# Small causal heads: transposed scores without a mask product, exponentials clipped on VectorE

## What is computed

```python
x = x + _L3_attn_a_ref(_layernorm(x), W_q, b_q, W_k, b_k, W_v, b_v, W_o, b_o)
x = x + _L3_ffn_ref(_layernorm(x), ...)
x = x + _L3_attn_b_ref(_layernorm(x), w_qkv, w_out)
x = x + _L3_ffn_ref(_layernorm(x), ...)

# inside _L3_attn_a_ref (b is the same without biases and rotation)
scores = jnp.einsum('bhtd,bhsd->bhts', q, k)
causal = jnp.tril(jnp.ones((t, t), dtype=bool))
mask = jnp.where(causal, 0.0, -jnp.inf)
probs = jax.nn.softmax((scores + mask) / jnp.sqrt(jnp.float32(dh)), axis=-1)
out = jnp.einsum('bhts,bhsd->bhtd', probs, v)
```

## Time and profile before

| | |
|---|---|
| median of 3 runs | 2899.02 us (2896.28 to 2901.09) |
| profiled execution, its own time | 2887.07 us |
| its span | 2885.8 us |
| mean granted TensorE clock | 0.892 |
| PE busy | 2243.0 us, 78% |
| DVE busy | 1824.5 us, 63% |
| ACT busy | 1345.5 us, 47% |

### The profile page before, as it was taken

The page is one execution under the profiler, slowest core; times in us unless marked ns, Lnnn a source line. Parts: engine busy times, 40 slices in busy tenths (PEclk is TensorE's granted clock), DMA queues, the critical chain, the costliest instruction groups (busy, mean ns, idle before and its releaser), DMA issues.

```text
span 2885.8 us, 40933 instructions
## 1 busy us (share of the span) xinstructions
PE 2243.0 (78%) x15598; PEld 1461.0 (51%) x15598; DVE 1824.5 (63%) x3594; ACT 1345.5 (47%) x2535; POOL 653.7 (23%) x610
## 2 busy tenths in 40 slices
PE   4868738665884887887798599676689889689888
PEld 1222328643872554555497278355454554454554
DVE  6989997898336996996847655663742432642331
ACT  4545313231334886886673564353443353344242
POOL 1737681313023221220091055000100100100000
PEclk9999969877886998998898699678799999899899
DMA  4000037502763111111000000002000000000000
GB/s 150 0 0 0 5 101 211 157 11 91 222 184 102 44 42 26 45 42 50 35 1 1 0 1 1 0 2 82 1 1 1 1 1 8 1 2 1 1 1 8
DMA packets 70709, 117.80 MB, mean 41 GB/s; under 512 B 9617, under 2 KB 46225, under 8 KB 70161
## 3 DMA queue, kind: packets, MB, share of 16 engines
q1 hardware_dynamic: 64112, 104.69, 12.1%
q0 software_dynamic: 4096, 8.40, 0.9%
q10 hardware_dynamic: 2304, 2.10, 0.3%
HBM read 84.61 MB, written 16.78 MB: 35 GB/s over the span
## 4 chain that ended last, share of the span: by engine, by line
PE 33%; DVE 11%; issue 4%; ACT 3%; DMA 1%; SPq 1%; POOL 1%; DVEq 0%; POOLq 0%; ACTq 0%
PE ps L148 29%; PE ps L157 4%; DVE wide_q L188 3%; SPq L231 1%; DMA ring<-lags 1%; DVE outT L194 1%; DVE conv L185 1%; DVE x L179 1%; DVE stats L203 1%; DVE stat L188 1%; POOL long L179 1%; DVE centred L179 0%; ACT L166 0%; ACT L165 0%; ACT k L166 0%
## 5 line engine op out<-in xcount | busy, mean ns | idle before, releaser
L185 DVE SCALAR_TENSOR_TENSOR conv<-conv_in,held_l1a,conv 128x512 f32<-128x512 f32 x288 | 238.0, 846 | 21.0 <-ACT conv L166 18.2
L179 POOL TENSOR_TENSOR long<-long,product 128x512 f32<-128x512 f32 x136 | 167.8, 1277 | 280.8 <-ACT product L166 280.3
L209 POOL MEMSET wide_q<- 128x1536 f32 x8 | 11.0, 1378 | 871.3 <-DVE stream_b L182 813.8
L179 POOL TENSOR_TENSOR part<-state,c_rows 128x512 f32<-128x512 f32 x128 | 161.0, 1284 | 72.3 <-issue 53.2
L179 POOL TENSOR_TENSOR qk<-conv,held_const 128x512 f32<-128x512 f32 x64 | 90.2, 1410 | 343.7 <-DVE conv L185 343.7
L148 PE MATMUL ps<-part,held_const 128*128 128x512 f32 x256 | 147.0, 658 | 13.2 <-POOL part L179 8.4
L188 DVE TENSOR_REDUCE wide_q<-ps 128x4 f32<-128x512 f32 (+1 forms) x128 | 113.8, 952 | 54.9 <-PE ps L148 54.9
L191 DVE TENSOR_TENSOR_SCAN state<-decay,ps 128x512 f32<-128x512 f32 x128 | 146.9, 1194 | 0.0
L166 ACT ACTIVATE probs<-ps 128x768 f32<-128x768 f32 x128 | 96.5, 808 | 91.0 <-PE ps L148 90.8
L166 ACT ACTIVATE grown<-ps,held_route 128x512 f32<-128x512 f32 x92 | 63.2, 687 | 122.9 <-PE ps L148 106.2
L179 DVE TENSOR_TENSOR x<-x,ps 128x512 f32<-128x512 f32 x44 | 30.1, 684 | 138.7 <-PE ps L148 131.6
(11 more groups left out here) (503 smaller groups left out, 6012.1 us busy)
## 6 DMA issues: line engine op xcount, KB each, us to landing
ring_a<-in_experts SPq DMA_DIRECT2D x46, 512.0 KB
ring_b<-in_experts SPq DMA_DIRECT2D x46, 512.0 KB
turned<-conv SPq DMA_DIRECT2D x256, 64.0 KB
ring<-lags SPq DMA_DIRECT2D x64, 128.0 KB
held_l3f<-in_l3f SPq DMA_DIRECT2D x1, 2824.0 KB
xg<-rows_x_a SPq DMA_DIRECT2D x10, 256.0 KB
xg<-rows_x_b SPq DMA_DIRECT2D x10, 256.0 KB
rows_y_a<-y SPq DMA_DIRECT2D x10, 256.0 KB, 5.4
```

Source lines behind the costliest of these rows:

```text
L179: return self.vector(self.real.tensor_tensor(out, a, b, op), columns(out), out, a, b)
L185: return self.vector(self.real.scalar_tensor_tensor(out, a, p, b, first, second), columns(out) + 60, out, a, b)
L209: return self.vector(self.real.memset(out, value), columns(out) // 2, out)
```

## The change

- In the transposed loop the four products `ps<-ident,after` of a unit are gone. The second set of score products closes the accumulation and raises `scores_t` for the odd heads.
- The exponentials of the two diagonal blocks of each head are therefore made without a mask. A new DVE operation after each exponential instruction (two per unit, each on two heads, 128x2x2x128 elements, in place in `probs`) takes the minimum with a constant tile that is 0 where the key is later than the query and 3e38 elsewhere. It raises the new semaphore `hidden`, and the mix waits for `hidden` instead of `exps`.
- In DVE's program the two minima of a unit stand ahead of its copy to `outT`.
- The constant tile is 128 columns more in the load of the group `l3a` (512 to 640 columns).
- The score loop keeps its mask products.

```diff
--- before.py
+++ after.py
@@ -2594,7 +2594,7 @@
     UNITS = GROUPS * SEQS
     KEYS = P + T
     L = Layer(m, NORM + "projected kept blank placed rotated v turned_k k_kept turned_q q_kept scores peak top turned_t "
-              "t_kept scores_t exps mixed mixed_kept oturned inverse normed yturned okept out biased")
+              "t_kept scores_t exps hidden mixed mixed_kept oturned inverse normed yturned okept out biased")
     s = L.s
     a = Arena(m, st.first, st.late_size)
     n_ = normalize(m, st, L, a, x, st.tok[:, :, :], st.xT[:, :])
@@ -2607,6 +2607,12 @@
 
     def unit(u):
         return u // SEQS, u % SEQS
+
+    def hide_later(lane, u, k):
+        yield lane.wait_ge(s.exps, 2 * u + k + 1)
+        diagonal = e.probs[:, u % 2, 2 * k:2 * k + 2, :].rearrange("p h (c n) -> p h c n", n=P)[:, :, 0:3:2, :]
+        keep = m.w.c_seen.unsqueeze(1).unsqueeze(1).to_broadcast([P, 2, 2, P])
+        lane.tensor_tensor(diagonal, diagonal, keep, ALU.min).then_inc(s.hidden)
 
     def tensor(pe):
         yield from n_.tensor(pe)
@@ -2666,16 +2672,12 @@
                           tile_position=(W * j, 0), skip_group_check=True)
             for j in range(HG):
                 r = slice(W * j, W * j + W)
-                pe.matmul(st.ps(j)[:, T:KEYS], b.kT[r, g, at + P:at + T], b.qT[r, g, at + P:at + T], start=False,
-                          stop=False, tile_position=(W * j, 0), skip_group_check=True)
-            for j in range(HG):
-                diagonal = st.ps(j)[:, 0:KEYS + P].rearrange("p (a n) -> p a n", n=T)[:, :, 0:P]
-                mm = pe.matmul(diagonal, m.after[:, :], m.ident16[:, :].unsqueeze(1).to_broadcast([P, 2, P]),
-                               start=False, stop=True, skip_group_check=True)
+                mm = pe.matmul(st.ps(j)[:, T:KEYS], b.kT[r, g, at + P:at + T], b.qT[r, g, at + P:at + T], start=False,
+                               stop=True, tile_position=(W * j, 0), skip_group_check=True)
                 if j % 2:
                     mm.then_inc(s.scores_t)
             yield pe.wait_ge(s.v, 1)
-            yield pe.wait_ge(s.exps, 2 * (u + 1))
+            yield pe.wait_ge(s.hidden, 2 * (u + 1))
             pr = e.probs[:, u % 2, :, :]
             for j in range(HG):
                 pe.matmul(st.ps(0)[W * j:W * j + W, 0:T], b.wide_v[:, TPS * q, HG * g + j, :], pr[:, j, 0:T],
@@ -2783,8 +2785,11 @@
             for i, (at, keys) in enumerate(((0, P), (P, T))):
                 ve.tensor_reduce(b.wide_q[:, TPS * q + i, HG * g:HG * g + HG, D], all_of(keys, at), X, ALU.max,
                                  negate=True).then_inc(s.peak)
+        yield ve.wait_ge(*m.loaded["l3a"])
         for u in range(UNITS):
             g, q = unit(u)
+            for k in range(2):
+                yield from hide_later(ve, u, k)
             yield ve.wait_ge(s.mixed, u + 1)
             ve.tensor_copy(e.outT[:, g, q * T:q * T + T], st.ps(0)[:, 0:T]).then_inc(s.mixed_kept)
         for g in range(GROUPS):
@@ -3193,7 +3198,8 @@
     g["rows"]["a_bout"] = v[n + "out_b"]
     n = "L3_attn_a_"
     g["l3a"] = {"c_qkv": _np.concatenate([v[n + "W_q"].T, v[n + "W_k"].T, v[n + "W_v"].T], axis=1),
-                "c_out": v[n + "W_o"].T}
+                "c_out": v[n + "W_o"].T,
+                "c_seen": _np.where(at[:, None] > at[None, :], 0.0, 3e38).astype(_np.float32)}
     g["rows"].update({"c_bqkv": _np.concatenate([v[n + "b_q"], v[n + "b_k"], v[n + "b_v"]]), "c_bout": v[n + "b_o"]})
     n = "L3_attn_b_"
     g["l3b"] = {"e_qkv": v[n + "w_qkv"].T, "e_out": v[n + "w_out"].T}
```

## The result

The changed kernel takes 2918.44 us (median of 6 runs, 2912.95 to 2924.2), the kernel before in the same comparison 2896.86 (6 runs, 2887.58 to 2901.09). The ratio is 1.0087, 95% interval 1.0068 to 1.0106: some 25 us slower by this ratio, 21.6 by the two medians. Ratios are of runs in the usual state alone, so one of the 19 runs of the kernel before beside e1 to e4, at 5634.62 us, is in none of them. The forecast was 2902, its range ended at 2918. The profiled execution took 2913.7 us with a span of 2912.4 and a mean granted clock of 0.882.

The account below looks back on a forecast made before the run. A PE-and-DVE ring was taken to bound the transposed loops, exponentials hidden beside it. Clock +2.4, edges -1.6 and +1.4, low clock carried into next blocks +0.8 sum to +3.0 us: 2890.1, or 2902 on the median's scale; range 2889 to 2918.

Parts of the forecast that it names:

- the clock's term: Transposed loops: PE's clock falls and returns, mean round 5.72 us against 5.63, times 25 rounds, +2.4 us.
- the ring: Transposed loops: the repeating chain bounding a two-unit round, 5.51 us instead of 5.63 at full clock; 25 rounds, -3.0 us.
- edges: Ends of the transposed loops: -1.6 us in the first stage, +1.4 us for units standing alone in the others.
- the tail: Stage four from stream b's first deep-network product to the end; the prediction booked no loss there.
- Cover has become the path: New round: scores b, four exponentials, one minimum, one mix bind; of 1.08 us mask removed, 0.12 is left as gain.
- The slow round: Transposed loops: a two-unit round with PE at half clock takes 7.10 us, 1.47 longer than the old one.
- I take one sixth: Transposed loops: one sixth taken at half clock, weighting rounds of 7.10 us against 5.51, mean 5.72.
- the second rival: Clock stays low for half of the loops or more: round 6.20 us at a half, 2915 us in all; chance 0.23.
- the slow loop itself keeps PE at 83%: Argument that the clock returns: in the slow round PE is busy 5.9 of 7.1 us.
- The first rival: The clock holds at 1.00 in the loops: -3.2 us, 2896 us, or 2889 if table loads count; chance 0.22.
- The shuffled merge: Moved merged order of blocks between stages two and three: a few us either way, within a case of chance 0.05.
- In old order: Transposed loops with minima but unchanged order: 2.36 us a unit, 0.45 less, 18 us over 41 steps; not booked.

Follow-up runs that it names:

- e1: Changed kernel plus nine unused identity products on PE per round of two units, between second stream's scores and first stream's mix; 2909.72 us, ratio 1.0103.
- e4: Changed kernel with the first two heads masked by a POOL product, the last two by DVE's minimum, in the old alternating order; 2930.66 us, ratio 1.0171.
- e5: Changed kernel plus five unused identity products on PE per round, behind stream a's score products; 2907.43 us, ratio 1.0039 to the kernel before.
- e3: Changed kernel, same order, each minimum on only 2 of 128 columns, so most of the mask is left out; 2876.06 us, ratio 0.9985.
- e2: Changed kernel with the planner pricing a minimum at nothing, so PE has the old alternating order with the same minima; 2887.0 us, ratio 1.002.
- e10: Changed kernel with all four mask products on PE, minima on 2 of 128 columns, planner's price of a minimum 1.0 us; 2864.69 us, ratio 0.9934.
- e7: Changed kernel with minimum for heads 0 and 1, mask product on PE for 2 and 3, minimum priced 1.0 us; 2862.02 us, ratio 0.9904; again 0.9901.
- e8: Changed kernel's order with the four mask products per unit kept on PE, minima on 2 of 128 columns, changing nothing; 2897.58 us, ratio 1.0013.

## Why the prediction was wrong

The forecast was 2902 us, 2918.4 was measured, and the step that failed is the clock's term. In the traces after the first copy the loss of 26.3 us is -3.0 for the ring, as forecast, 18.9 for the low clock, which e5 takes away, 5.2 left for the loops' edges (forecast -0.2), 8.3 in the tail (forecast 0) and -3.1 between.

- **The ring at full clock: right.** 5.51 us forecast, 5.51 in the changed kernel while the clock was up, and in the steady rounds of e5. Cover has become the path: the chain runs through exponential, minima, mix a and scores b, and e3 shows that one minimum of the four is on it. The minimum is 0.69.
- **The slow round: nearly right.** 7.10 forecast, 6.90 measured. I had scores a at half clock to their end, 3.27 us after the start of scores b, and a's exponentials waiting for them. They ended at 2.50, so four exponentials ran on end in 2.92. Mix b, which I had at half clock too, had the fast one, off the path.
- **"I take one sixth": the step that failed.** I turned a share of low clock into a share of slow rounds one to one, as if low clock fell evenly on work and waiting. It fell on the work. The slow round (2143.9 to 2150.8) is at half clock for half of its 6.9 us only, and yet it costs the whole price, 1.39 us, since all of mix a and scores b lies in that half. So a share of low clock makes twice that share of slow time. The share itself was too small as well, but this counts for less: over the four loops the mean clock was 0.82, 0.89, 0.93 and 0.91, which is 23% of their time at half where I had 17%. In my formula 23% gives +4.4 us instead of +2.4; twice 23% gives +13. The trace has 15 slow bursts in the four loops (6, 4, 2 and 3), some only in part; at 1.39 each they are at most 21 us, and e5 took 18.9 out of the loops, as many as 13.6 whole ones. My +2.4 should have been about +16: -3.0 and 19.
- **The argument against the second rival** ("the slow loop itself keeps PE at 83%") didn't help. The clock does come back after each slow burst, and so it did here: in the pause behind it, where nobody needs it. A loop can be slow in every round without the clock ever staying low.
- **The first rival's reason** (the gap of 1.5 is below the 1.92 that the earlier trace rows show) did not protect the clock: the clock fell at 2144.0 after PE waits of 1.73 and 0.55. The Trainium skill, "TensorE: Matmul & The Clock Gate", section "HAM oscillation — how this bites in real kernels", shows a loop that starts each burst at the low clock, behind long waits for loads. The trace agrees with the picture, but here the waits are for exponentials and minima, and short.
- **Edges: wrong in the first stage.** I booked -1.6 by the last copy, stream a's. What the next block waits for is stream b's. In e5, at full clock, b's last copy comes 38.5 us after the first copy, 39.4 before, as seven rounds of 0.12 less make it. But b's deep network starts 13.4 us behind it and not 12.0, since now both streams turn and normalise at the same time: PE waits 2.82 us for DVE's `stream_b` where it waited 1.04. Over four stages the loops of e5 are 2.2 above before where my terms (-3.0 - 1.6 + 1.4) give -3.2. The first stage's 1.4 is traced; of the rest, the fourth stage has one burst at half clock behind its last round (2801.3 to 2804.7), and what remains is open.
- **The tail: not foreseen.** The shuffled merge had a chance of 0.05 and "a few us either way", and I looked for it between stages two and three. In stage four it cost 8.3 us, a third of the loss, and was to be read in the new order: one more unit of stream a behind the start of stream b's deep network, and behind its 14 us of products.
- **The second rival** was the right mechanism, with 14 or 15 of 25 rounds slow ("half of the loops or more"): it gave 2915. With the tail's 8.3 and the 3.1 got back between it would have been 2920, a loss of 21 us; 2918.4 was measured, and by the traces after the first copy the loss is 26.3. The rest is the edges, which the forecast and this rival had at nearly nothing.
- **"In old order" 18 us to gain**: e2 shows that this was too bright. The second minimum is 0.27 late in the ring, in the first stage DVE's order makes a minimum the copy's rival, and the clock falls there too, for 13.6 us on end.

## What to carry to other kernels

When work is taken off PE, ask what the pause it leaves does to the granted clock, and price the low clock where PE's work lies and not as a share of time: a loop of burst and pause can have the low clock in each burst and the high one in each pause. If a mask can be done early on one engine or late on another, split it by who is early: that took 16 us out of the loops against the whole mask on PE with the blocks in nearly the same order (e10 to e7), between a third and a half of e7's 1%. The rest came from the order alone. So compare the order of the blocks around a loop as carefully as the loop; one leftover unit behind another stream's block cost a third of this loss.

## Unexpected of the hardware

The alternation of the clock locks to the loop: low for the burst, high for the pause, in every round from 2144 to the end of the stage, and gone with 1.38 us of products in the pause (e5), with 0.5 us less waiting in the round (e3) or with the mask back (e8). In the old order with the same work taken off PE (e2) the low clock does not alternate but holds for 13.6 us on end, with PE busy 83% of them. DVE's minimum with both sources in SBUF takes 1.15 us while POOL runs a product of the same size, 0.69 alone (e4). The Trainium skill, "GPSIMD Engine Reference", names this pair in its table: the SBUF interfaces are shared with VectorE, with contention for DVE instructions that have two SBUF inputs. The trace agrees.

Open is why what lies ahead of the first stage differs by up to 28 us between profiled executions of the same instructions.
